# A decoder layer on one core: the chosen half of the tokens fetched and written back by row index instead of by one-hot products

## What is computed

```python
x = x + attn(layernorm(x))                    # stage a: causal linear attention, 16 heads
x = x + xattn(layernorm(x), ctx, ctx)         # stage b: divergence attention over ctx, norm, MLP of 1024, norm
x = x + ffn(layernorm(x))                     # stage c

def ffn(x):                                   # stage c
    scores = x @ w_router
    _, idx = top_k(scores, 128)               # half of the 256 tokens of a batch
    x_sel = take_along_axis(x, idx)           # in order of rank
    qkv = rmsnorm(x_sel, g1) @ W_qkv.T        # causal softmax attention among the chosen, 16 heads
    x_attn = softmax(mask(q k.T / 4)) v @ W_out.T
    h2 = rmsnorm(x_sel + x_attn, g2)
    x_ff = silu(h2 @ W1.T) * (h2 @ W2.T) @ W3.T
    return x.at[idx].set(x_sel + x_attn + x_ff)
```

## Time and profile before

| what | value |
|---|---|
| median of 3 runs | 952.1 us (951.48 to 952.46) |
| span of the profiled execution | 947.8 us; the page gives no other time of it |
| TensorE busy | 883.4 us, 93% |
| VectorE busy | 727.6 us, 77% |
| ScalarE busy | 595.2 us, 63% |
| GpSimd busy | 218.6 us, 23% |
| chain that ended last | TensorE 64%, VectorE 20%, ScalarE 7%, issue 7%, DMA 1% |
| one round in the middle | 54.40 us |
| table loads of ScalarE | 4 a round, 1.28 us each |
| filler products | 164, 46.7 us busy |

### The profile page before, as it was taken

The page is one execution under the profiler, slowest core; times in us unless marked ns, Lnnn a source line. Parts: engine busy times, 40 slices in busy tenths (PEclk is TensorE's granted clock), DMA queues, the critical chain, the costliest instruction groups (busy, mean ns, idle before and its releaser), DMA issues.

```text
span 947.8 us, 21833 instructions
## 1 busy us (share of the span) xinstructions
PE 883.4 (93%) x7652; PEld 750.3 (79%) x7652; DVE 727.6 (77%) x1670; ACT 595.2 (63%) x1582; POOL 218.6 (23%) x379
## 2 busy tenths in 40 slices
PE   7888999999999999999999999999999999998987
PEld 4657797978879797887979788787979788786855
DVE  4878878787887878888787879788787878866342
ACT  4365757667574767657575766757576675745533
POOL 0215122121313122221312222231321222121100
...
DMA packets 20465, 25.05 MB, mean 26 GB/s; under 512 B 1488, under 2 KB 18000, under 8 KB 20432
## 3 DMA queue, kind: packets, MB, share of 16 engines
...
...
## 4 chain that ended last, share of the span: by engine, by line
PE 64%; DVE 20%; ACT 7%; issue 7%; DMA 1%; POOL 0%; DVEq 0%; SPq 0%; ACTq 0%; POOLq 0%
PE bank L1064 21%; PE bank L1370 4%; PE bank L1166 4%; PE bank L1356 4%; PE bank L1331 3%; PE bank L1245 3%; PE bank L1253 3%; PE bank L1424 2%; DVE before L950 2%; ACT L615 2%; PE bank L1319 2%; PE bank L1184 2%; PE bank L1457 2%; PE bank L1080 2%; DVE prob L850 2%
## 5 line engine op out<-in xcount | busy, mean ns | idle before, releaser
L652 ACT ACTIVATE w_raw_or_stage_c<-bank,c_nmax 128x128 f32<-128x128 f32 x256 | 90.6, 375 | 12.3 <-DVE c_nmax L981 12.3
L615 ACT ACTIVATE prob<-bank,b_folded 128x256 f32<-128x256 f32 x128 | 53.7, 471 | 46.0 <-PE bank L1064 45.8
L981 DVE TENSOR_REDUCE c_nmax<-bank 128x4 f32<-128x512 f32 x64 | 43.5, 683 | 48.1 <-PE bank L1356 48.1
L809 DVE TENSOR_TENSOR a_s<-bank,const 128x512 f32<-128x512 f32 x112 | 71.8, 677 | 9.0 <-PE bank L1166 6.4
L729 DVE TENSOR_TENSOR b_s_lo<-prob,b_s_hi 128x512 fp32r<-128x512 f32 x64 | 54.2, 848 | 27.3 <-ACT b_s_hi L503 27.3
L426 POOL TENSOR_TENSOR a_tr_lo<-a_norm,a_tr_hi 128x512 fp32r<-128x512 f32 x16 | 21.0, 1310 | 216.9 <-ACT a_tr_hi L503 216.9
L402 POOL TENSOR_TENSOR x<-x,vectors_by_row 128x512 f32<-128x512 f32 x16 | 20.7, 1292 | 161.7 <-DVE w_raw_or_stage_c L975 161.7
L652 ACT ACTIVATION_READ_ACCUMULATOR w_raw_or_stage_c<-bank,c_nmax 128x1 f32 x256 | 55.1, 215 | 0.0
L799 DVE RECIPROCAL a_e<-a_e 128x512 f32<-128x512 f32 x16 | 53.4, 3340 | 0.0
L1064 PE MATMUL bank<-b_s_hi,w_mlp_hi 128*128 128x256 f32 x256 | 44.8, 298 | 4.8 <-ACT prob L615 4.6
L1475 PE MATMUL bank<-ones_bf 128*128 128x512 bf16 x164 | 46.7, 410 | 1.0 <-POOL ones_bf L400 1.0
...
## 6 DMA issues: line engine op xcount, KB each, us to landing
x_in<-in_x SPq DMA_DIRECT2D x16, 256.0 KB, 2.7
qc<-in_ctx SPq DMA_DIRECT2D x16, 256.0 KB, 3.2
b_f<-in_ctx_t SPq DMA_DIRECT2D x16, 256.0 KB, 3.4
out<-w_raw_or_stage_c SPq DMA_DIRECT2D x16, 256.0 KB, 2.1
...
```

The lines of the kernel that those rows point to most:

```text
L615: act_in(prob[:, 2 * (j % 2) + n, :], b0[:, n * T:(n + 1) * T], ACT.Gelu, bias=b1p[:, f:f + 1]).then_inc(b_gelu.sem, 1)
L652: act_in(c_e[g % 2][:, j * R:(j + 1) * R], (c1, c2)[g % 2][:, j * R:(j + 1) * R], ACT.Exp, bias=c_nmax[:, n:n + 1], accum_out=c_den[:, hea ...
L809: tt(heads(A_MASKED[t][n][:, :]), heads(A_SCORES[n][:, :]), tri.unsqueeze(1).broadcast_to([P, 4, P]), ALU.mult).then_inc(a_scput.sem, 1)
L981: nc.vector.tensor_reduce(c_nmax[:, 4 * g:4 * g + 4], heads((c1, c2)[g % 2][:, :]), axis=AX.X, op=ALU.max, negate=True).then_inc(c_max.sem, 1)
```

## The change

- The rows that stage c needs (c_norm, x2 and the rms factor, 513 numbers) lie in one tile `rows` and SyncE stores all 256 of them to a DRAM tensor `token_rows` (`store_rows`).
- The rank of a token is counted by VectorE alone: one instruction for each half compares bank c0 with the token's score and adds up along the row (`c_rank`, L994). The tie rule is in a bound that is 0 or minus the least normal number.
- A one-hot matrix in bf16 times the token numbers (c_idx, TensorE, L1345) gives the token of each rank; it is copied to an index tile (c_idxput).
- c_pick (GpSimd, L509) fetches the 128 chosen rows by index. c_hsc (VectorE, L1012) scales them, c_ht (TensorE, L1352) transposes them.
- c_ob is x2 + c_norm for all tokens, on GpSimd (L500), and is stored before the chosen ones are known. c_xo loses its first product; c_h2put is a VectorE addition of x_sel, c_h2sq the squares on ScalarE. c_hx (GpSimd) adds x2 of the chosen, c_y adds the MLP's result, c_put (GpSimd, L525) writes the 128 rows into `out` by index. c_yhi, c_ylo, c_scat, c_done are gone.
- `preload_act_table_set` ahead of a_qout names a set that has both exp and ln: two table loads a round in place of four.
- `ORDER` is another list, and `WARM_AT` is empty; the 14 products at the start remain.

The core of the diff:

```diff
 ORDER = """
...
-c_mean a_tlo c_y+ b_tanhq c_ff_1+ b_v b_pnorm c_ylo+ c_yhi+ b_vput c_normed a_q c_scat+ a_k a_qout c_sbc
...
+b_dput c_sel c_idxput c_sbc c_ff_0+ b_dtp+ c_idx b_qb b_rput b_vq c_ff_1+ b_ratio b_rtp a_phi_q a_ktp a_phi_k
...
+WARM_AT = {}
...
+            def store_rows(b):
+                sp.wait_ge(*c_normed(b))
+                sp.sem_inc(passed.sem, 1)
+                sp.wait_ge(*c_rms1(b))
+                sp.sem_inc(passed.sem, 1)
+                if not first(b):
+                    sp.wait_ge(*picked_in(b - 1))
+                    sp.sem_inc(passed.sem, 1)
+                sp.dma_start(token_rows_by_p, rows[:, :, 0:W]).then_inc(rows_out.sem, 16)
...
+            with sp.Fori(2, B - 1) as i:
+                next_ctx(i - 1)
+                store_rows(i - 2)
+                store(i - 2)
+                next_ctx_t(i - 1)
                 next_x(i)
...
+            def c_ob_(b):
+                pool.wait_ge(*c_normed(b))
+                if not first(b):
+                    pool.wait_ge(*out_done(b - 1))
+                nc.gpsimd.tensor_tensor(ob[:, :, :], x2, c_norm, ALU.add).then_inc(c_ob.sem, 1)
+
+            def c_pick_(b):
+                pool.wait_ge(*c_idxput(b))
+                pool.wait_ge(*rows_out(b))
+                if not first(b):
+                    pool.wait_ge(*c_hx_s(b - 1))
+                    pool.wait_ge(*c_h2put(b - 1))
+                pool.sem_inc(passed.sem, 1)
+                nc.gpsimd.indirect_dma_start(
+                    picked[:, 0:W], None, token_rows[:, :], bass.IndirectOffsetOnAxis(ap=index[:, 0:1], axis=0)) \
+                    .then_inc(picked_in.sem, 16)
...
+            def c_put_(b):
+                pool.wait_ge(*c_y(b))
+                pool.wait_ge(*c_kept(b))
+                pool.wait_ge(*out_done(b))
+                pool.sem_inc(passed.sem, 1)
+                nc.gpsimd.indirect_dma_start(
+                    out[:, :], bass.IndirectOffsetOnAxis(ap=index_out[:, 0:1], axis=0), y_out, None) \
+                    .then_inc(y_stored.sem, 16)
...
             def a_qout_(b):
+                nc.scalar.preload_act_table_set("natural_log_exp_and_others")
...
+            def c_rank_(b):
                 dve.wait_ge(*c_sbc(b))
+                for t in range(TT):
+                    if t:
+                        dve.wait_ge(*c_rank(b, t))
+                    stt(tie[:, :], c0[:, 0:T], c_sc[:, t:t + 1], tie_bound[:, t, :], ALU.subtract, ALU.is_gt,
+                        accum_out=c_rk[:, t:t + 1]).then_inc(c_rank.sem, 1)
...
+                for t in range(TT):
+                    dve.wait_ge(*c_rank(b, t + 1))
+                    ts(sel[:, t, :], iota_bf[:, :], c_rk[:, t:t + 1], None, ALU.is_equal).then_inc(c_sel.sem, 1)
...
+            def c_hsc_(b):
+                dve.wait_ge(*picked_in(b))
+                ts(c_h[:, :], x_sel, r1_sel, None, ALU.mult).then_inc(c_hsc.sem, 1)
...
             def c_ht_(b):
-                pe.wait_ge(*c_sels(b))
+                pe.wait_ge(*c_hsc(b))
+                pe.wait_ge(*c_idxput(b))
                 for c in range(DC):
-                    for t in range(TT):
-                        last = mm(c0[:, c * R:(c + 1) * R], c_norm[:, t, c * P:(c + 1) * P], sel_s[:, t, :],
-                                  start=t == 0, stop=t == TT - 1)
+                    last = nc.tensor.transpose(c0[:, c * R:(c + 1) * R], c_h[:, c * P:(c + 1) * P], ident)
...
             def c_xo_(b):
-                pe.wait_ge(*c_selu(b))
                 pe.wait_ge(*c_dput(b))
-                for t in range(TT):
-                    mm(c2[:, 0:D], sel[:, t, :], c_norm[:, t, :], start=t == 0, stop=False, skip_group_check=True)
```

More of the change, by code:

```diff
@@ L42 @@
 ORDER = """
[L43 to L47, removed]
@@ L53 @@
-c_etput_1 a_score_1 b_htp b_fnormed a_att_0 c_etp_2 c_exp_2 c_w8 a_scput_4 b_hhi c_max_3 b_hlo c_rstd c_rms1
-a_scput_5 a_scput_6 c_dinv b_up_0 a_scput_7 c_exp_3 c_etput_2 c_etp_3 a_dinv c_dtp c_dbc c_etput_3 b_glo_0
-b_gelu_0 b_ghi_0 c_w9 a_att_1
+b_ghi_0+ b_gelu_1+ c_dtp+ b_up_1+ c_dput+ b_ghi_1+ a_rstd c_o+ c_att+ b_down_0+ b_up_2+ c_w2 a_yhi+ b_rstd
+b_gelu_2+ c_h2sq+ a_mean b_glo_1+ c_w3 c_xo+ a_proj+ b_ghi_2+ c_h2put+ b_up_3+ a_done+ b_gelu_3+ c_h2tp+
+b_down_1+ a_normed b_mean b_glo_2+ c_gu_0+ b_down_2+ c_h2lo+ c_h2hi+ b_ghi_3+ b_tanhk b_glo_3+ c_gate_0+ c_w0
@@ new lines @@
+c_tanh_0+ c_w4 b_down_3+ c_h2rms+ c_hx+ c_tanh_1+ c_gu_1+ b_normed b_o+ a_thi b_omean+ c_gthi_0+ b_tanhq
+c_gu_2+ c_gate_1+ b_onormed+ c_gthi_1+ c_gtp_0+ b_done+ b_v c_mean a_tlo c_gtlo_0+ b_orstd+ c_rstd b_vput
+b_pnorm c_normed c_rms1 a_qout c_rscore a_tp c_gtp_1+ b_log c_gtlo_1+ a_q a_kout b_diff c_rank a_k a_val
+b_dput c_sel c_idxput c_sbc c_ff_0+ b_dtp c_idx b_qb b_rput b_vq c_ff_1+ b_ratio b_rtp a_phi_q a_ktp a_phi_k
+a_csum b_sid c_pick a_vput c_ob c_y+ a_kput c_hsc a_kq c_w5 c_ht c_hput a_state c_put+ a_sput b_kept b_sexp
@@ L56 @@
+c_max_0 c_max_1 c_qk a_den c_w6 c_qkput b_fput b_fmean b_fb2 b_frstd c_score_0 a_kept a_scput_0 a_scput_1
+a_scput_2 b_fd a_mask a_dput c_exp_0 b_fnormed c_v c_exp_1 a_score_0 c_vput a_scput_3 c_etp_0 c_w7 c_etput_0
+c_max_2 c_score_1 c_etput_1 c_max_3 b_hhi a_scput_4 c_w1 c_etp_1 c_exp_2 a_ylo b_hlo b_htp a_score_1 c_exp_3
+a_att_0 c_etput_2 c_w8 a_scput_5 c_dinv c_etp_2 c_dbc a_scput_6 b_gelu_0 a_scput_7 c_keep a_dinv b_glo_0
+c_etput_3 b_up_0 c_etp_3 a_y a_att_1 c_w9
 """.split()
@@ L679, in c_h2hi_ @@
                 copy(flat(c_hs[0][:, :, :]), c0[:, 0:D], c_h2hi)
-            def c_yhi_(b):
-                act_e.wait_ge(*c_y(b))
-                copy(flat(c_hs[0][:, :, :]), c_h2[:, :], c_yhi)
             def c_tanh_(j):
@@ L1346, in step @@
                         pe.wait_ge(*c_qkput(b))
-                        pe.wait_ge(*c_selu(b))
+                        if not first(b):
+                            pe.wait_ge(*c_y(b - 1))
                     else:
```

214 lines of the change are left out of this document (92 added, 122 removed).

## The result

The changed kernel takes 1003.9 us (median of 4 runs, 996.4 to 1007.1) against 952.3 us of the kernel before on the same chip: ratio 1.0535, 95% interval 1.0506 to 1.0564. I had forecast 943 with a range up to 976. It is slower by 5.4%.

What follows compares the result with a forecast made beforehand. TensorE was taken as the bound, though pausing for VectorE from b_o to the ranking's end. The profiled 947.8 us less 23.8 over 14 rounds, plus 14.8 at start and end, plus 4.3 to the median, gave 943; range 922 to 976.

Steps and rivals of the forecast that it cites:

- The step that failed first: c_ob on GpSimd (1.29 us) takes 0.87 off VectorE where it waited anyway; b_qb's move was given no cost.
- Rival 3: GpSimd's descriptor writing held off by VectorE from b_vq to c_y, gather 4 us late: 1007 us; chance 0.03.
- The detour: Chosen rows through DRAM: store 3.0 us, landed D+12.5, hidden behind the index; gather 4.0, landing D+17.05 as VectorE reaches c_hsc.
- no slack: At c_hsc: each us of the gather beyond 4.1 costs a us on every round.
- rival 2: Row fetch late, 6.6 us: 983 us; total turns positive with lateness L above 0.56, a gather over 4.6 us; chance 0.15.
- The index: VectorE's path from b_o's start (D): the index of chosen rows is in SBUF at D+13.05.
- the 52.7: Forecast length in us of a middle round, 1.7 shorter than the 54.40 before; -23.8 over 14 rounds.
- The two waits that I did add: New TensorE waits each round: c_etp_0 some 0.4 us, b_htp ahead of a_score_1 0.45 us.
- TensorE's work: Work leaving TensorE, from rank products, compaction, row copy and scatter less c_idx: 2.95 us a round.
- Rival 4: Clock falls inside each middle round behind crowded TensorE pauses, 1.5 us a round comes back: 964 us; chance 0.12.
- Start and end: First and last stretches, without 150 fillers and with the detour open: +14.8 us, bounds 0 and +25.
- Tables: Two exp/ln table loads saved, 2.6 us of ScalarE a round, count at nothing: ScalarE idles 18 us a round.

Runs made afterwards that it cites:

- experiment 3: Also written e3_both: changed kernel with GpSimd's additions b_qb back behind b_o and c_ob made to wait for c_hput; 972.4 us (1.0209).
- experiment 8: e3_both with the row store in two halves, x2 sent as soon as b_done is through, then the normalised rows with their scale; 962.9 us (1.0124).
- experiment 7: e3_both with c_hsc scaling the first 128 normalised rows from SBUF, not the fetched (wrong rows used), all transfers still issued; 950.3 us (0.9989).
- experiment 4: Changed kernel with 8 filler products, results unused, in front of c_sbc in every round but the first; 993.4 us (1.0435).
- experiment 11: The kernel before with only the table set holding both exp and ln loaded ahead of a_qout; 952.2 us against 951.5 (1.0009).

## Why the prediction was wrong, step by step

**The step that failed first** is the one that moves b_qb and c_ob on GpSimd: c_ob on GpSimd "takes 0.87 off VectorE in a place where VectorE waited anyway", and b_qb's move from D+0.8 to D+8.5 (D is the start of b_o, as in the prediction), which I did not cost at all. I asked whether GpSimd had time for its additions, not what VectorE was doing beside them. What came in its place: c_norm, sums and phi step held, 34.5 us more of VectorE, and 31.5 us of time (experiment 3). The Trainium skill (SBUF — State Buffer, Who interferes with whom), on the very list from which I took the line on descriptor writing, says that a VectorE instruction with two SBUF inputs contends with a GpSimd instruction that reads SBUF, and that tensor_scalar can too. The traces agree: the phi step, the sums and b_s_lo are held (two inputs in SBUF), and so is c_norm (tensor_scalar), while in e3_both the gate's step with one input in a bank keeps its length beside b_qb (0.47, as before's 459 ns).

**Rival 3** (0.03) looked at the same pair of engines from the other side, with GpSimd's descriptors held by VectorE. I let it fall by the skill, and wrongly so: in e3_both the fetch takes up to 1.58 instead of 1.09 and ends with the phi step of k. But it is 0.5 us at most, not 4, and no large part of the loss.

**The detour.** c_normed was to end at D+9.0 and the rows to be stored at D+12.5, half a us before the index. In the short round c_normed ends at D+10.24, 1.2 late by the hold, and the fetch starts 5.25 behind it, not 3.5: the store of 513 KB lands in 3.9 where I took 3.0. So the fetch starts at D+15.5 instead of 13.05, and c_ht comes 2.4 late. I had written that there is no slack; what was late did come through. The fetch took the 4.0 forecast only if it is counted from its start on GpSimd to c_hsc, and that is luck, since the 4.0 were to begin at the index: 0.8 to 1.0 passes between what releases it and that start, and 4.7 from index to rows (experiment 8), where rival 2 set the turning point at 4.6. Rival 2 (0.15) is thus the mechanism of what e3_both has left: its formula with L = 1.2, the round's price by experiment 7, gives 14(1.2 - 1.7) + 14.8 + 2.4 = +10 over 952, 962, beside 972. By the Trainium skill (DMA: Bandwidth & Descriptors, Anatomy of one DMA) the fetch was estimated at 2.6; the profile gives 3.6 from issue to landing, and the measurement decides. Price of the trip 22 us (experiment 7).

**The index** was right: D+13.05 forecast, D+12.9 in e3_both, where VectorE is not held.

**Waits not seen.** a_q waits 0.36 and 0.40 each round for a_tr_hi and a_tr_lo, since b_v and a part of c_ff, which stood between a_tp and a_q, are elsewhere now; I had no term for that. With it and c_score_0's 0.34, the 52.7 becomes 53.8, beside 53.5 in experiment 7. The two waits that I did add, 0.4 and 0.45, came to 0.81, but all of it in front of a_att_0, and nothing before c_etp_0.

**TensorE's work.** I took 2.95 off; its busy time fell by 2.0 (51.88 to 49.91). Part may be that an instruction behind a pause does not overlap the one before; that was not tested.

**The clock.** Rival 4 (0.12) was partly right: the lower level came in five of the middle rounds, behind c_sbc's wait, a_ktp's or both, and took 10 us in all (experiment 4). These 10 are part of the 31.5, since both waits are long by the holds.

**Start and end** came to +17.6 against +14.8: near by luck, for other reasons. I gave 12.5 to the clock; fillers gave back 5.0 in the tail and nothing ahead of it. The trip alone makes 6 of the tail; the rest of it was not taken apart.

**Tables** at nothing, right (experiment 11).

Downward from the measured 1003.9, holds 31.5 and trip 22 leave the 950.3 of experiment 7. The 7 us between that and 943 are the difference of rounds that are 0.8 longer than forecast and ends that are shorter; they were not taken apart further. The trip was in the forecast, but hidden in the rounds; the hold not at all.
